# Expanding the heads in eight transfers of 72 rows instead of twelve of 24

## The reference

```python
y = layernorm(x) * ln_w + ln_b
q, k, v = (einsum('bsd,hde->bhse', y, w) for w in (wq, wk, wv))     # 16 heads of 8
scores  = einsum('bhse,bhte->bhst', q, k) / sqrt(8) + causal_mask
attn    = softmax(scores) @ v                                       # per head, then heads side by side
x = layernorm(x + (attn @ wo + x))
x = layernorm(x + (x @ (W + up_aux @ lora_up @ lora_down @ down_aux).T + b))
```

## Time and profile before

| | |
|---|---|
| profiled execution, device time | 445.28 us |
| its span, first to last instruction | 443.6 us |
| mean granted TensorE clock | 0.988 |
| TensorE busy | 416.9 us, 94% |
| VectorE busy | 382.5 us, 86% |
| ScalarE busy | 339.4 us, 77% |
| GpSimd busy | 306.2 us, 69% |
| moved by DMA | 69.16 MB, mean 156 GB/s |

### The profile page before, as it was taken

One profiled execution on the slowest core, in us unless ns is written; L12 is line 12 of the kernel. 1 busy time (PEld: TensorE's weight loads), 2 busy tenths in 40 slices (PEclk: granted clock), 3 DMA queues, 4 the chain that ended last, 5 costly groups with the idle time before them and its releaser, 6 DMA issues.

```text
span 443.6 us, 15833 instructions
## 1 busy us (share of the span) xinstructions
PE 416.9 (94%) x5571; PEld 332.1 (75%) x5571; DVE 382.5 (86%) x1056; ACT 339.4 (77%) x865; POOL 306.2 (69%) x395
## 2 busy tenths in 40 slices
PE   6698999989999997989999999999999999999993
PEld 3356678868888886878888888888888888876662
DVE  4589978988999897989998999999999999988664
ACT  2376777778888886877888888888888888876871
POOL 6754857775677777676777777777777778744663
PEclk9699999999999999999999999999999999999998
DMA  2556575656676657677576776667666665555111
GB/s 75 157 166 173 152 200 145 156 137 161 192 187 158 183 151 162 146 177 195 146 178 174 169 165 182 166 172 191 182 186 169 174 183 164 154 151 131 52 38 38
DMA packets 77915, 69.16 MB, mean 156 GB/s; under 512 B 9307, under 2 KB 68530, under 8 KB 77874
## 3 DMA queue, kind: packets, MB, share of 16 engines
q1 hardware_dynamic: 76446, 67.68, 58.5%
q10 hardware_dynamic: 1428, 0.95, 0.9%
HBM read 47.07 MB, written 21.00 MB: 153 GB/s over the span
## 4 chain that ended last, share of the span: by engine, by line
PE 65%; DMA 9%; DVE 9%; SPq 7%; ACT 5%; issue 4%; POOL 0%; DVEq 0%; ACTq 0%; POOLq 0%
PE pv_bank L1369 14%; PE bank L1382 7%; PE bank L1377 7%; PE score_bank L1347 6%; PE max_bank L1330 5%; PE max_bank L1326 5%; PE max_bank L1332 5%; DVE rowmax L1041 5%; DMA kx<-k_rows 5%; PE score_bank L1350 4%; PE score_bank L1346 4%; PE bank L1439 2%; PE bank L1440 2%; DMA qx<-mT 2%; SPq L296 2%
## 5 line engine op out<-in xcount | busy, mean ns | idle before, releaser
L1041 DVE TENSOR_REDUCE rowmax<-max_bank 128x2 f32<-128x512 f32 (+1 forms) x384 | 245.6, 676 | 22.8 <-PE max_bank L1332 15.9
L617 ACT ACTIVATE probs<-score_bank 128x384 f32<-128x384 f32 x512 | 223.8, 498 | 41.3 <-PE score_bank L1351 38.4
L512 POOL TENSOR_SCALAR_AFFINE_SELECT probs<-probs 128x1024 f32<-128x1024 f32 x127 | 137.7, 1093 | 82.7 <-ACT probs L617 82.6
L1369 PE MATMUL pv_bank<-probs,v_ext 128*32 128x256 f32 x2032 | 97.5, 329 | 0.0
L1347 PE MATMUL score_bank<-qx,kx 74*128 74x256 bf16 x324 | 85.0, 271 | 0.0
L1369 PEld LDWEIGHTS pv_bank<-probs,v_ext 128*32 128x32 f32 x2032 | 56.4, 109 | 32.2 <-issue 6.6
L1330 PE MATMUL max_bank<-kx,qx 128*128 128x128 bf16 x512 | 71.0, 220 | 2.7 <-DVE rowmax L1041 2.3
L1346 PE MATMUL score_bank<-qx,kx 74*128 74x128 bf16 x324 | 70.0, 220 | 2.9 <-DMA qx<-mT 2.9
L1332 PE MATMUL max_bank<-kx,qx 74*128 74x128 bf16 x512 | 70.7, 219 | 0.0
L1330 PEld LDWEIGHTS max_bank<-kx,qx 128*128 128x128 bf16 x512 | 42.3, 98 | 18.0 <-DVE rowmax L1041 6.0
L1326 PE MATMUL max_bank<-kx,qx 128*128 128x128 bf16 x512 | 49.9, 219 | 5.5 <-DMA kx<-k_rows 5.0
(11 more groups left out here) (127 smaller groups left out, 679.7 us busy)
## 6 DMA issues: line engine op xcount, KB each, us to landing
kx<-k_rows SPq DMA_DIRECT2D x187, 96.0 KB
qx<-q_rows SPq DMA_DIRECT2D x128, 96.0 KB
qx<-q_rows SPq DMA_DIRECT2D x64, 104.0 KB
q_rows<-parts SPq DMA_DIRECT2D x32, 192.0 KB, 2.2
k_rows<-parts SPq DMA_DIRECT2D x31, 192.0 KB, 2.4
xa<-in_x SPq DMA_DIRECT2D x32, 128.0 KB, 3.7
xr<-in_x SPq DMA_DIRECT2D x32, 128.0 KB, 2.2
out<-y SPq DMA_DIRECT2D x32, 128.0 KB, 3.2
```

Of the source, the lines that this page charges most:

```text
L512: pool.affine_select(out=t, in_=t, compare_op=ALU.is_ge, fill=0.0, base=0, pattern=[[0, GROUP * NB], [1, P]], channel_multiplier=-1)\
L617: act.activation(probs[:, h, 0:PW], score_bank[SCORE_BANK[h]][:, 0:PW], ACT.Exp, scale=SCALE / Q_SCALE)\
L1041: dve.tensor_reduce(to, of, AX.X, ALU.max).then_inc(s_mread[unit], 1)
L1369: ins = pe.matmul(pv_bank[VW * g:VW * g + VW, n * P:SEQ], v_ext[r][:, n, head(h), window], probs[:, h, 0:SEQ] if n == 0 else probs[:, h, S ...
```

## The change

The twelve expansion transfers of a batch become eight: four sets of four heads (`SETS`, `SET`), and in each set one transfer of queries and one of keys, each of 72 rows x 4 heads, as 72 blocks of 2 KB. The three turns become the outermost step of the source's access pattern: with step 0 for the queries (the same 24 rows three times), with a step of 8 rows for the keys. The destination is 72 partitions in one run. The zeros for rows 72 and 73 no longer come with the third turn: a transfer of their own (`clear_max_rows`) copies them from a tile in SBUF at the head of `expand`; the zero rows in DRAM and the stores that make them are gone. The two transfers of max rows become one over two partitions. TensorE waits before units 0, 3, 6 and 9, each time for its set. The engines' orders of compute instructions, TensorE's with the first maxima unit directly behind the two groups of `pv` that open a step, are the same as before.

```diff
+SETS = 4
+SET = HEADS // SETS
-        q_rows = [nc.dram_tensor(f"q_rows{i}", [(PART_ROWS + MAX_PARTS) * HEADS, SEQ], BF16).ap() for i in range(2)]
+        q_rows = [nc.dram_tensor(f"q_rows{i}", [PART_ROWS * HEADS, SEQ], BF16).ap() for i in range(2)]
-        EXPAND = 16 * 2 * PARTS
+        EXPAND = [16 * 3] + [16 * 2] * (SETS - 1)
-        MAX_ROWS = 16 * MAX_PARTS
+        def heads_of(number):
+            return slice(number * SET, number * SET + SET)
+        def queries_of(number, parity):
+            t = q_rows[parity]
+            return bass.AP(tensor=t.tensor, offset=number * SET * SEQ,
+                           ap=[[0, PARTS], [HEADS * SEQ, PART_ROWS], [1, SET * SEQ]])
+        def keys_of(number, parity):
+            t = k_rows[parity]
+            return bass.AP(tensor=t.tensor, offset=number * SET * SEQ,
+                           ap=[[HD * HEADS * SEQ, PARTS], [HEADS * SEQ, PART_ROWS], [1, SET * SEQ]])
-            def store_zero_rows():
-                sp.wait_ge(s_zero, 1)
-                for rows_of in q_rows:
-                    sp.dma_start(rows_of[PARTS * P:, :], zero_rows[:, :]).then_inc(s_zero, 16)
+            def clear_max_rows(slot):
+                sp.dma_start(qx[slot][SPLIT_ROWS:SCORE_ROWS, :, :], zero_rows[:, :]).then_inc(s_expand[0], 16)
             def expand(it, o):
...
-                for half in range(HALVES):
-                    heads = slice(half * HALF, half * HALF + HALF)
-                    if half == 0:
+                r, p = it.ring(o), it.parity(o)
+                clear_max_rows(r)
+                for number in range(SETS):
+                    if number == 0:
                         sp.wait_ge(s_q_stored, it.done(o, 16))
                     else:
-                        sp.wait_ge(s_expand[1], it.done(o - 1, EXPAND))
-                    for turn in range(PARTS):
-                        a, n = turn * PART_ROWS, PART_ROWS + (MAX_PARTS if turn == PARTS - 1 else 0)
-                        sp.dma_start(qx[r][a:a + n, heads, :], q[0:n, heads, :]).then_inc(s_expand[half], 16)
-                    if half == 0:
+                        sp.wait_ge(s_expand[number], it.done(o - 1, EXPAND[number]))
+                    sp.dma_start(qx[r][0:SPLIT_ROWS, heads_of(number), :], queries_of(number, p))\
+                        .then_inc(s_expand[number], 16)
+                    if number == 0:
                         sp.wait_ge(s_stored, it.done(o, STORES))
-                    for turn in range(PARTS):
-                        a = turn * PART_ROWS
-                        sp.dma_start(kx[r][a:a + PART_ROWS, heads, :],
-                                     k[turn * HD:turn * HD + PART_ROWS, heads, :]).then_inc(s_expand[half], 16)
+                    sp.dma_start(kx[r][0:SPLIT_ROWS, heads_of(number), :], keys_of(number, p))\
+                        .then_inc(s_expand[number], 16)
             def load_max_rows(it, o):
                 sp.wait_ge(s_mT, it.done(o))
-                for part in range(MAX_PARTS):
-                    sp.dma_start(qx[it.ring(o)][SPLIT_ROWS + part:SPLIT_ROWS + part + 1, :, :],
-                                 mT[part * HEADS:(part + 1) * HEADS, :]).then_inc(s_mrow, 16)
+                sp.dma_start(qx[it.ring(o)][SPLIT_ROWS:SCORE_ROWS, :, :], mT[:, :]).then_inc(s_mrow, 16)
...
-                if unit % (UNITS // HALVES) == 0:
-                    pe.wait_ge(s_expand[unit // (UNITS // HALVES)], it.done(o, EXPAND))
+                if unit % (UNITS // SETS) == 0:
+                    number = unit // (UNITS // SETS)
+                    pe.wait_ge(s_expand[number], it.done(o, EXPAND[number]))
```

More of the change, by code:

```diff
@@ L188, in build @@
         s_const = sem("constants_made")
-        s_zero = sem("zero_rows_made_and_stored")
+        s_zero = sem("zero_rows_made")
         s_vfill, s_ones, s_mask_made = sem("v_ext_filled"), sem("ones_made"), sem("mask_rows_made")
@@ L202, in build @@
         s_q_stored, s_stored = sem("q_stored"), sem("k_stored")
-        s_expand = sems("heads_expanded_half", HALVES)
+        s_expand = sems("heads_expanded_set", SETS)
         s_v, s_vx = sem("v_in_bank6"), sem("v_ext_ready")
@@ L287, in store_parts @@
                 if it.static:
-                    sp.wait_ge(s_expand[0], it.done(o - 2, EXPAND))
-                    sp.wait_ge(s_expand[1], it.done(o - 2, EXPAND))
+                    for number in range(SETS):
+                        sp.wait_ge(s_expand[number], it.done(o - 2, EXPAND[number]))
                 p3 = it.done(o)
@@ L305, in expand @@
                 alone(sp, "sp")
[L306 to L309, removed]
-                for half in range(HALVES):
-                    heads = slice(half * HALF, half * HALF + HALF)
-                    if half == 0:
+                sp.wait_ge(s_expand[0], it.done(o - 1, EXPAND[0]))
+                r, p = it.ring(o), it.parity(o)
@@ L326, in store_first_queries @@
             def store_first_queries():
                 sp.wait_ge(s_p3q, 1)
[L328 to L347, removed]
+                sp.dma_start(q_rows[0].rearrange("(i p) s -> p i s", p=P), parts[:, :, 0, :]).then_inc(s_q_stored, 16)
+            def expand_first_queries():
+                sp.wait_ge(s_zero, 1)
+                sp.wait_ge(s_slot[0], 2)
+                clear_max_rows(0)
+                sp.wait_ge(s_q_stored, 16)
+                for number in range(SETS):
+                    sp.dma_start(qx[0][0:SPLIT_ROWS, heads_of(number), :], queries_of(number, 0))\
+                        .then_inc(s_expand[number], 16)
@@ L368, in first @@
                 store_first_queries()
-                expand_first_queries(0)
-                expand_first_queries(1)
-                expand_first_keys_turn()
+                expand_first_queries()
                 load_xa(at, 3)
@@ L621, in copy_maxT @@
                 if it.static:
-                    act.wait_ge(s_mrow, it.done(o - 1, MAX_ROWS))
+                    act.wait_ge(s_mrow, it.done(o - 1, 16))
                 act.wait_ge(s_mTp, it.done(o))
@@ L657, in store_first_keys, with expand_first_keys @@
                                   parts[:, 0:n, 1, :]).then_inc(s_stored, 16)
[L659 to L663, removed]
-                k = k_rows[0].rearrange("(r h) s -> r h s", h=HEADS)
-                for turn in range(PARTS - (half == 0)):
-                    a = turn * PART_ROWS
-                    act.dma_start(kx[0][a:a + PART_ROWS, heads, :], k[turn * HD:turn * HD + PART_ROWS, heads, :])\
-                        .then_inc(s_expand[half], 16)
+            def expand_first_keys():
+                act.wait_ge(s_slot[0], 2)
+                act.wait_ge(s_stored, STORES)
+                for number in range(SETS):
+                    act.dma_start(kx[0][0:SPLIT_ROWS, heads_of(number), :], keys_of(number, 0))\
+                        .then_inc(s_expand[number], 16)
             def fill_queries(slot):
@@ L728, in first @@
                 copy_v(at, 0)
-                expand_first_keys(0)
-                expand_first_keys(1)
+                expand_first_keys()
                 first_parts(at, 1)
@@ L1339, in scores @@
                 if h == 0:
-                    pe.wait_ge(s_mrow, it.done(o, MAX_ROWS))
+                    pe.wait_ge(s_mrow, it.done(o, 16))
                 last = last_in_bank(h)
```

3 lines of the change are left out of this document (1 added, 2 removed).

## The result

The changed kernel takes 727.26 us (median of 4 runs, 726.71 to 727.89), the kernel before beside it 447.12 us: ratio 1.627, interval 1.618 to 1.637. The direction and the mechanism were those of the forecast; the size was not: 832 us was forecast, with 745 as the lower end.

A forecast was written before the change was run, and what follows sets the result against it. TensorE bound the kernel before; three DMA engines would bound the changed one. 17.2 + thirty-one periods of 24.3 (22.0 + 2.3), 753.3, + 19.5 + 40 + 1.7 gave 832 us; range 745 to 985.

The forecast's parts named there:

- the mechanism: In the expansion, each transfer confined to few engines, so the DMA share there would not stay over 0.5.
- Three engines, and the same three: Outermost counts 3 and 72 put each of the eight expansion transfers on three engines, always the same, thirteen standing still.
- The price of the expansion: 393,216 bytes on each of three engines at 21.9 GB/s, the least crowded window's price: 18.0 us a batch.
- The other estimate: Expansion at the skill page's 27 GiB/s for one engine: 13.6 us, period 19.9, whole about 692 us.
- The rest of the traffic: Other loads and stores on the three engines: 3.1 us, plus 0.9 for clearing and max rows, each batch.
- the gap: Between batches, the next expansion waits for its batch's stores: 2.3 us (bounds 1 and 4).
- Start and tail: First keys' expansion issued at 17.2 us; last expansion drains in 19.5; then 40 us to the end.
- TensorE keeps up: From the queue's draining to the stores' issue takes 12.4 us, under 20, so the three engines set the period.
- rival D: TensorE idles, the clock is granted at half, perhaps 27.5 us a period: 956 us; chance 0.12.
- Rival A: Expansion spread over up to sixteen engines, waits for keys and perhaps max rows gone: 437 us; chance 0.05.
- Issues: nothing: On SP, twelve issues of about 0.39 us become nine; cost nothing, at most 0.6 us either way.
- The range: Total time for 8 in 10: 745 to 985 us, holding the forecast's own range, D and C's nearer part.

The follow-up runs named there:

- experiment 1: The changed kernel with the two outer steps of the source patterns swapped, 24 rows outermost and the three turns inside: 454.75 us, 1.020 of the kernel before.
- Experiments 4, 5 and 6: Changed kernel: 256 KB load added ahead of stores 751.89 us, behind 727.92; query store last 752.46 us; input load and output store moved behind stores 710.33 us.

## Why the prediction was wrong, point by point

**Three engines, and the same three.** Right; shown by experiment 1 and by the counts of updates. That they are the same three each time is shown by the queueing (share 0.17 with eight transfers queued); which three, no run shows. The rows of before had no transfer with different outermost counts, so this was an inference, and it held.

**The price of the expansion, 18.0 us a batch.** It was 17.4. Off by 0.6 a step, 19 us in all. The other estimate, by the Trainium skill's 27 GiB/s, was too low: 13.6 us for the expansion (its terms add up to 691 us, not 692).

**The rest of the traffic, 4.0, and the gap, 2.3.** This is the step that failed: these two terms were added up as if one came behind the other, and the runs show that they overlap. The sum of 6.3 us measured 3.7. I added the whole of the other traffic and then the whole of the latency, "of that about 1 us is the data moving, counted above". But only the blocks up to the query store stand in the way (input, output, max rows, query store: 16 + 16 + 16 + 24 = 72 blocks of 0.027 us, 1.9 us, where an engine has a share in each). The key stores, the residual load and the clearing move while the landing is seen, the next transfer issued and its first block under way (1.5 us from the issue at 371.26; I had taken 0.7, and in the kernel before it was mostly 0.9 for 24 rows when nothing was queued). Experiments 4, 5 and 6 show it: traffic ahead of the query store costs its engine time (+24.6 for 24), behind it nothing (+0.7), and the order alone moves the total by +25 and -17 us. The two terms together were too large by 2.6 us a step, 81 of the 105 us.

**Start and tail.** 17.2 for 15.2 (the queries' expansion begins before the keys'), 19.5 for 17.9 and 40 for 37.7, the last as suspected there: 6 us.

**TensorE keeps up.** Right. The clock (rival D) did fall, to 0.82 in the mean and to 0.50 in the gap's window above, and TensorE was busy 495.9 us instead of 416.9. In the steps it cost nothing: between 100 and 600 us SP waited for the maxima for 0.2 us in all, so TensorE was never late there, and experiments 4 to 6 move the total by transfers alone, with the clock at 0.81 to 0.83 in each. From the last block of expansion to the end it was 37.7 us, 36.9 in the kernel before, so hardly anything there either.

**Rival A's saving.** It would have been 437 us with the expansion spread; experiment 1 spread it and got 455. The waits for the keys did go (5.0 to 0.8 us), but those for the max rows, which were perhaps to go too, rose from 2.9 to 11.5. "Issues: nothing" was wrong: I priced an issue at 0.39 us, and one of these takes 0.75.

**The range.** Its lower end of 745 stands for a period of 21.5 us. The period without the double counting, by the price of the forecast (18.0 + 1.9 + 1.8 = 21.7, the 1.8 being the measured 3.7 less 1.9), would have given 751, and with the expansion at 17.4 and the measured start and tail 727. No value in the range let the two terms overlap.

## What to carry to other kernels

Before merging transfers, write down the outermost count of both access patterns as the instruction carries them: here each transfer ran on the largest number of engines, up to 16, that divides both (3, 12, 13, 2), so a loop of three copies belongs inside the rows, not outside. To price a store-then-load loop, split the traffic at the transfer whose landing lets the next go; what is queued ahead of it adds up, what is queued behind it hides in the latency, as far as the latency reaches. Time the issue of each form of transfer in a trace, since here it ranged from 0.39 to 0.75 us; on a queue that also carries the critical transfer one issue less can be worth microseconds.

## What was not expected of the hardware

- A queue backs up on its issuer: the first six expansion transfers were issued in 0.68 to 0.95 us each, the seventh took 2.74 and the eighth 1.91 us. With twelve engines at work (experiment 1) 95 in 100 of these issues took 0.75 to 0.84 us, so it was the backlog of the three engines that held SP.
- Blocks of 4 KB took 0.171 us with three engines at work and 0.251 in the mean with twelve; 2 KB blocks 0.090 with three and 0.101 with twelve, over the whole kernels.
- An expansion issue took 0.39 us for 24 rows and 0.75 for 72, whether of 2 or 4 KB. Neither rows nor blocks alone set this price: the query store, over 128 rows and in 384 blocks, was issued in 0.43 us, a load of the max rows over one row in 0.58 and over two in 0.69. The 72-row form also has one step more in its source pattern, and no run parts this from the rows.
